# A fused attention, state-space and expert kernel on one core: expert selection moved into the first stage

## What is computed

```
x = x + xattn(layernorm(x), ctx)      # q, k from ctx; softmax(q k^T); x_m = logits attention^T
x = x + ffn16(layernorm(x))           # router scores -> top 2 of 16 experts per token, silu(g) * u, down
x = x + mamba(ctx, layernorm(x))      # in_proj, conv of 4 taps, silu, dt = softplus(...), scan over tokens
x = x + ffn8(layernorm(x))            # two experts of 8, chosen for all tokens

scores = x @ router_w                 # [tokens, 16]
routing_weights, routing_idx = top_k(softmax(scores), 2)   # then normalised to sum 1
dt = softplus(dt_low @ dtp_w + dtp_b)
state = state * exp(dt * A) + (dt * u) * B_t ;  y = sum(state * C_t)
```

## Time and profile before

| | |
|---|---|
| median of 3 runs | 1596.34 us (1596.19, 1596.34, 1598.69) |
| the profiled execution | span 1594.7 us; what lies around a span is not shown by the profile, the median is 1.6 us above it |
| busy share of the span | PE 87%, weight loads 65%, DVE 59%, ACT 45%, POOL 49% |
| chain that ended last, by engine | PE 58%, DVE 22%, issue 10%, ACT 4%, POOL 3%, DMA 3% |
| 0 to 250 us, first stage | 58 us for a batch |
| 250 to 294.5 us, sort | PE idle but for 2 us, DVE busy |
| from 294.5 us | scans and experts, then the third and fourth layer |

### The profile page before, as it was taken

One profiled execution on the slowest core, in us unless ns is written; L12 is line 12 of the kernel. 1 busy time (PEld: TensorE's weight loads), 2 busy tenths in 40 slices (PEclk: granted clock), 3 DMA queues, 4 the chain that ended last, 5 costly groups with the idle time before them and its releaser, 6 DMA issues.

```text
span 1594.7 us, 18873 instructions
## 1 busy us (share of the span) xinstructions
PE 1391.5 (87%) x6080; PEld 1030.4 (65%) x6080; DVE 936.9 (59%) x1186; ACT 709.8 (45%) x1303; POOL 784.0 (49%) x607
## 2 busy tenths in 40 slices
PE   6988983588899989897166999999999999999998
PEld 3535532566666656664166787878787887878786
DVE  2677767999999999998683224241414224241413
ACT  4445433266766776665143333333333333333332
POOL 0000000788888988885631445444544545444442
PEclk9898895699999999999555999999999999999999
DMA  3202214477977987863655900010000100010000
GB/s 105 108 26 81 107 53 165 158 240 257 315 257 234 319 269 264 281 198 125 218 198 203 364 14 0 0 66 1 14 0 13 52 13 0 0 53 0 0 0 26
DMA packets 78202, 191.29 MB, mean 120 GB/s; under 512 B 10856, under 2 KB 15752, under 8 KB 77120
## 3 DMA queue, kind: packets, MB, share of 16 engines
q1 hardware_dynamic: 64832, 157.03, 29.3%
q0 software_dynamic: 6400, 20.98, 4.1%
q10 hardware_dynamic: 6912, 12.59, 2.2%
HBM read 152.55 MB, written 38.01 MB: 119 GB/s over the span
## 4 chain that ended last, share of the span: by engine, by line
PE 58%; DVE 22%; issue 10%; ACT 4%; POOL 3%; DMA 3%; ACTq 0%; SPq 0%; DVEq 0%; POOLq 0%
PE decay L1675 22%; PE bank L1664 21%; DVE decay L1247 11%; DVE S L1256 4%; PE bank L1474 2%; PE decay L1430 2%; PE bank L1437 1%; DVE XH L1114 1%; PE bank L1494 1%; PE bank L1534 1%; PE decay L1484 1%; PE bank L1619 1%; POOL Y L767 1%; PE bank L1561 1%; PE decay L1480 1%
## 5 line engine op out<-in xcount | busy, mean ns | idle before, releaser
L1387 DVE CAST HFH<-HF 128x512 fp32r<-128x512 f32 x128 | 59.0, 461 | 496.7 <-ACT HF L1045 496.7
L815 POOL TENSOR_TENSOR W2L<-W2R,W2H 128x512 fp32r<-128x512 f32 x128 | 172.5, 1347 | 348.2 <-ACT W2H L1040 348.2
L728 POOL TENSOR_TENSOR S<-DTU,Bb 128x1024 f32<-128x1024 f32 x128 | 304.7, 2401 | 25.1 <-DVE row_hot L1229 21.7
L1247 DVE TENSOR_TENSOR_SCAN decay<-decay,S 128x1024 f32<-128x1024 f32 x128 | 292.9, 2288 | 0.5 <-ACT decay L892 0.5
L1664 PE MATMUL bank<-XSH,W1H 128*128 128x512 f32 x512 | 202.9, 396 | 4.2 <-POOL W1L L811 4.2
L1675 PE MATMUL decay<-W2H,HFH 128*128 128x512 f32 x512 | 200.4, 391 | 5.3 <-DVE HFL L1389 5.3
L1664 PE MATMUL bank<-XSH,W1L 128*128 128x512 f32 x512 | 203.0, 396 | 0.0
L1664 PE MATMUL bank<-XSL,W1H 128*128 128x512 f32 x512 | 202.3, 395 | 0.0
L1675 PE MATMUL decay<-W2L,HFH 128*128 128x512 f32 x512 | 199.9, 390 | 0.0
L1675 PE MATMUL decay<-W2H,HFL 128*128 128x512 f32 x512 | 199.7, 390 | 0.0
L811 POOL TENSOR_TENSOR W1L<-W1R,W1H 128x512 fp32r<-128x512 f32 x128 | 171.1, 1337 | 49.6 <-ACT W1H L1031 49.6
(11 more groups left out here) (212 smaller groups left out, 2102.3 us busy)
## 6 DMA issues: line engine op xcount, KB each, us to landing
WGU<-in_L_ffn_gate_w SPq DMA_DIRECT2D x48, 384.0 KB, 3.8
WGU<-in_L_ffn_up_w SPq DMA_DIRECT2D x48, 384.0 KB, 5.1
WD<-in_L_ffn_down_w SPq DMA_DIRECT2D x48, 384.0 KB, 4.9
Bb<-bc_rows SPq DMA_DIRECT2D x32, 512.0 KB, 7.9
Cb<-bc_rows SPq DMA_DIRECT2D x32, 512.0 KB, 9.7
expert_rows<-YT ACTq DMA_DIRECT2D x48, 256.0 KB, 4.2
W1R<-in_L_ffn_w SPq DMA_DIRECT2D x6, 1024.0 KB, 13.9
W2R<-in_L_ffn_w SPq DMA_DIRECT2D x6, 1024.0 KB, 14.1
```

What stands on the lines that cost most here:

```text
L728: pool.tensor_tensor(S[u % NP][:], DTU[:, ds(b, 1), c, :].to_broadcast([P, PAIR, L]), Bb[j][:], ALU.mult).then_inc(dbu_ready, 1)
L815: pool.tensor_tensor(W2L[f % 2][:], W2R[:, ds(e, 1), f, :].rearrange("p e d -> p (e d)"), W2H[f % 2][:].bitcast(F32), ALU.subtract).then_i ...
L1247: dve.tensor_tensor_scan(flat, flat, S[u % NP][:].rearrange("p i l -> p (i l)"), 0.0, ALU.mult, ALU.add).then_inc(scan_done, 1)
```

## The change

- Selection of experts for a batch (top 2, OH, MM, diff) is a function `select(b)`. It is run for batches 0, 1 and 2 in the following batch, between `softmax` and `convolve`, and for batch 3 behind the stage.
- DVE's hardware loop over batches is written out.
- bn_stats of a tile is taken between the additions of x, not behind all four.
- In batch 3 ACT takes the scores ahead of Exp; DVE runs select(3), then softplus(3) without DT and DTU, which come as `step_sizes(3)` behind rf and ahead of row_hot.
- The 16 additions of totals become one `tensor_tensor_scan` with a mask `reset` that is zero at each expert's first tile; PE writes the totals in the order expert, tile.
- SP loads the row pairs 0 to 3 of batch 0 (B and C, eight transfers) in batch 3, two pairs behind `qk_ready`, two behind the turning of the probabilities; U and the pairs 4 to 7 follow where the loads were.
- POOL makes its constants ahead of its waits, and starts the units at `hot_ready` 2, the first product for tile_hot.
- Buffers are allocated in another order, so that the early rows land on the memory of ctxT and XN.

```
@@ transfers (SP)
             def sequence_transfers(b, last):
+                if last:
+                    sp.wait_ge(qk_ready, B)
+                    sp.wait_ge(bc_stored, DMA + DMA)
+                    first_rows(0)
+                    first_rows(1)
+                    sp.wait_ge(t_ready, (B - 1) * 12 + 2 * T)
+                    first_rows(2)
+                    first_rows(3)
                 sp.wait_ge(u_ready, b + 1)
...
-            for j in range(NP):
-                load_b(0, j)
-                load_c(0, j)
-                if j < DC:
-                    load_u(0, j)
+            for j in range(DC):
+                load_u(0, j)
+            for j in range(HP, NP):
+                first_rows(j)
@@ POOL
-            pool.wait_ge(score_copied, B)
-            pool.wait_ge(x1_stored, B * DMA + DMA)
-            pool.wait_ge(xn1_stored, B * DMA + DMA)
-            pool.wait_ge(bc_stored, B * DMA + DMA)
-            pool.wait_ge(dt_ready, B)
...
+            pool.memset(reset[:, :, 0:1], 0.0).then_inc(const_ready, 1)
...
-            pool.wait_ge(hot_ready, 1)
+            pool.wait_ge(x1_stored, B * DMA + DMA)
+            pool.wait_ge(xn1_stored, B * DMA + DMA)
+            pool.wait_ge(bc_stored, B * DMA + DMA)
+            pool.wait_ge(dt_ready, B)
+            pool.wait_ge(hot_ready, 2)
             for u in range(AHEAD):
                 dbu(0, u)
@@ ACT
+            def take_scores(b):
+                wait_apart(act, score_ready, b + 1)
+                act.copy(SC[:, ds(b * T, T), :], PS[6][:, 0:T * E].rearrange("p (t e) -> p t e", t=T)
+                         ).then_inc(score_copied, 1)
...
+                if last:
+                    take_scores(b)
                 act.wait_ge(abs_ready, b * DC + DC)
                 act.activation(ZZ[:], ZZ[:], ACT.Exp, scale=-1.0).then_inc(z_ready, 1)
...
+                if not last:
+                    take_scores(b)
...
-            act.wait_ge(diff_ready, 1)
+            act.wait_ge(diff_ready, B)
@@ DVE
+            def step_sizes(b):
...
+                step.mark(dve.tensor_tensor(DT[:, b], RL[:], ZZ[:], ALU.add))
                 step.wait()
+                dve.tensor_tensor(DTU[:, b], DT[:, b], U[:], ALU.mult).then_inc(dt_ready, 1)
...
+            def select(b):
+
+                ts = slice(b * T, (b + 1) * T)
+                dve.wait_ge(score_copied, b + 1)
+                for t in range(T):
+                    ins = dve.max(M8[:, t, :], SC[:, b * T + t, :])
+                do(ins)
+                for t in range(T):
+                    ins = dve.max_index(I8[:, t, :], M8[:, t, :], SC[:, b * T + t, :])
+                dve.tensor_tensor(diff[:, ts].rearrange("p (t o) -> p t o", o=1), M8[:, :, 1:2], M8[:, :, 0:1],
+                                  ALU.subtract).then_inc(diff_ready, 1)
+                do(ins)
+                for k in range(TOP):
+                    ins = dve.tensor_copy(IF[:, k, :].rearrange("p (t o) -> p t o", o=1), I8[:, :, k:k + 1])
+                do(ins)
+                dve.wait_ge(const_ready, 4)
+                for k in range(TOP):
+                    ins = dve.tensor_tensor(OH[:, k, ts], iota_e[:]..., IF[:, k, :]..., ALU.is_equal)
+                do(ins)
+                dve.tensor_tensor(MM[:, ts], OH[:, 0, ts], OH[:, 1, ts], ALU.add).then_inc(mask_ready, 1)

             def sequence_dve(b, last):
                 softmax(b)
+                if b:
+                    select(b - 1)
                 convolve(b)
...
+                add_x(0)
+                add_x(1)
+                measure(0)
+                measure(1)
+                add_x(2)
+                measure(2)
+                add_x(3)
+                step.mark(measure(3))
                 dve.wait_ge(xn1_stored, b * DMA + DMA)
+                layernorm(X1A, XN1, b * 2 + 2, var_ready, rstd_ready, xn1_ready, measured=True)
                 positive_part(b)
                 if not last:
                     layernorm_x(b + 1)
-                softplus(b)
+                    softplus(b)
+                    step_sizes(b)

             layernorm_x(0)
-            with step.loop(B - 1, 3 * DC + 2 + 4 + 2 * T) as b:
-                sequence_dve(b, False)
-            sequence_dve(B - 1, True)
+            for b in range(B):
+                sequence_dve(b, b == B - 1)
+
+            select(B - 1)
+            softplus(B - 1)
...
-            do(dve.memset(PX[:, 0, :], 0.0))
-            totals = DOWN[:, 0:NT * E].rearrange("p (t e) -> p t e", t=NT)
-            for t in range(NT):
-                do(dve.tensor_tensor(PX[:, t + 1, :], PX[:, t, :], totals[:, t, :], ALU.add))
+            do(dve.tensor_tensor_scan(PX[:].rearrange("p e t -> p (e t)"), reset[:].rearrange("p e t -> p (e t)"),
+                                      DOWN[:, 0:NT * E], 0.0, ALU.mult, ALU.add))
...
             do(dve.scalar_tensor_tensor(rf[:], jf[:], -float(P), posf[:], ALU.mult, ALU.add))
+            step_sizes(B - 1)
             dve.tensor_tensor(row_hot[:], iota_r[:]..., rf[:]..., ALU.is_equal).then_inc(hot_ready, 1)
@@ PE
-            pe.matmul(DOWN[:, 0:NT * E], ones[:], MM[:].rearrange("p t e -> p (t e)"), start=True,
-                      stop=True).then_inc(rank_ready, 1)
+            pe.matmul(DOWN[:, 0:NT * E].rearrange("p (e t) -> p e t", e=E), ones[:], MM[:].rearrange("p t e -> p e t"),
+                      start=True, stop=True).then_inc(rank_ready, 1)
```

More of the change, by code:

```diff
@@ L183, in build_program @@
-        q.close()
+        PR = sb(s, "PR", [P, T, L])
+        QKT = sb(s, "QKT", [P, 2, L])
+        X1A = sb(s, "X1A", [P, T, DM])
+        XN1 = sb(s, "XN1", [P, T, DM])
+        XP = sb(s, "XP", [P, DC, L + TAPS - 1])
+        RL = sb(s, "RL", [P, DC, L])
+        ND = sb(s, "ND", [P, DC, L])
+        ZZ = sb(s, "ZZ", [P, DC, L])
+        XH = sb(s, "XH", [P, DC, L])
+        xdb = sb(s, "xdb", [XD, L])
+        XB = sb(s, "XB", [P, T, DM])
+        XNT = sb(s, "XNT", [P, K, L])
+        ATT = sb(s, "ATT", [P, K, L])
@@ L184, in build_program @@
+        MM = sb(s, "MM", [P, NT, E])
         s.close()
         m = ExitStack()
+        BC = [[sb(m, f"Bb{j}", [P, PAIR, L]), sb(m, f"Cb{j}", [P, PAIR, L])] for j in range(HP)]
         S = [sb(m, f"S{j}", [P, PAIR, L]) for j in range(NP)]
[L188 to L189 removed]
+        BC += [[sb(m, f"Bb{j}", [P, PAIR, L]), sb(m, f"Cb{j}", [P, PAIR, L])] for j in range(HP, NP)]
+        Bb, Cb = [bc[0] for bc in BC], [bc[1] for bc in BC]
@@ L702, in _ @@
             rstd_of(2 * B, var_ready, rstd_ready)
-            pool.wait_ge(score_copied, B)
-            pool.wait_ge(x1_stored, B * DMA + DMA)
-            pool.wait_ge(xn1_stored, B * DMA + DMA)
-            pool.wait_ge(bc_stored, B * DMA + DMA)
-            pool.wait_ge(dt_ready, B)
-            pool.affine_select(out=tri[:], in_=ones[:], compare_op=ALU.is_gt, fill=0.0, base=0,
+            step.mark(pool.memset(tri[:], 0.0))
+            step.mark(pool.memset(reset[:], 1.0))
+            step.wait()
+            pool.affine_select(out=tri[:], in_=tri[:], compare_op=ALU.is_gt, fill=-1.0, base=0,
                                pattern=[[1, P]], channel_multiplier=-1).then_inc(const_ready, 1)
+            pool.memset(reset[:, :, 0:1], 0.0).then_inc(const_ready, 1)
             pool.iota(iota_j[:], pattern=[[1, SLOT_TILES]], base=0, channel_multiplier=0,
@@ L1061, in _, with layernorm @@
             dve.wait_ge(small_loaded, SMALL_LOADS * DMA)
[L1062 to L1067, removed]
+            def layernorm(src, dst, count, ready, got, done, measured=False):
+                if not measured:
+                    for t in range(T):
+                        ins = dve.bn_stats(stats[:, t, :], src[:, t, :])
+                    step.mark(ins)
+                step.wait()
                 for t in range(T):
@@ L1126, in softplus @@
             def softplus(b):
-                dt, dtu = (a_[:, ds(b, 1)].rearrange("p b c l -> p (b c) l") for a_ in (DT, DTU))
                 dve.wait_ge(z_ready, b + 1)
@@ new lines, in do @@
+            def do(ins):
+                step.mark(ins)
+                step.wait()
+            def select(b):
[4 more added lines that the diff above has]
+                do(ins)
+                for t in range(T):
+                    ins = dve.max_index(I8[:, t, :], M8[:, t, :], SC[:, b * T + t, :])
[7 more added lines that the diff above has]
+                for k in range(TOP):
+                    ins = dve.tensor_tensor(OH[:, k, ts], iota_e[:].rearrange("p (o e) -> p o e", o=1).to_broadcast([P, T, E]),
+                                            IF[:, k, :].rearrange("p (t o) -> p t o", o=1).to_broadcast([P, T, E]),
+                                            ALU.is_equal)
+                do(ins)
+                dve.tensor_tensor(MM[:, ts], OH[:, 0, ts], OH[:, 1, ts], ALU.add).then_inc(mask_ready, 1)
```

127 lines of the change are left out of this document (45 added, 82 removed).

## The result

The changed kernel takes 1598.58 us (median of 17 runs, 1595.94 to 1600.95). The kernel before, timed beside it on the same chip, takes 1594.20 us (17 runs, 1588.29 to 1598.69). The ratio is 1.0025, with a 95% interval of 1.0015 to 1.0035: slower by 2.4 to 5.6 us, the middle just above the 0.2% that I had called the least that can be told. The forecast was 1596.1 us and "within 0.2%". The time lies in the range, the sign does not agree.

What follows compares the result with a forecast made beforehand. No engine is busy throughout; the first stage's and sort's chain of waits decides. Tail -10.7, selection +5.7, clock +3.4, router +1.4 give -0.2: 1594.7 - 0.2 + 1.6 = 1596.1 us, own range 1593 to 1599, wider range 1591 to 1600.

Steps and rivals of the forecast that it cites:

- Selection, 1.9 us a batch: First stage: selection between softmax and convolution delays PE by 1.9 us in batches 1 to 3, +5.7 us in all.
- New wait of 2.6 us, falls of 1.7 us, two of three: Attention: PE idles 2.6 us before its second half; the clock falls, 1.7 us each, in two of three batches, +3.4.
- 5.7 + 3.4 = 9.1: First stage: 5.7 us for three selections on PE's path and 3.4 us for two falls of the clock.
- Router, +1.4: Last batch's router: its products take 4.09 us or 7.01 at half clock, now on the path; the middle, +1.4 us.
- Tail, -10.7: Sort, from the last router's end to the first scan: R + 33.6 in place of R + 44.3, -10.7 us.
- R: The end of the router's products in the last batch, 250.21 us before, from which the tail is counted.
- the bound that I did not take: tile_hot to first scan: upper bound of 3.7 us, if the second product goes before POOL's first S; 2.7 was taken.
- Statistics, order on ACT: First stage: bn_stats between the additions gain nothing; last batch: scores before Exp put softplus at R + 3.6, selection hidden.
- First rows, "nothing": SP's loads in batch 3: eight transfers moved ahead of u_spill, none on the path, so worth nothing.
- rival 3: Second stage's start: the gather behind eight S becomes the bound, up to 4.2 us later against the scans; 1598.2, chance 0.10.
- my half of 4.2 us, +2.1: Second stage's start: half of the gather's largest delay against the scans, 1596.1 + 2.1 = 1598.2 us.
- Rival 4: Sort: tile_hot takes 9.95 us even without POOL beside it, for its own cause; +7.0 us, 1603, chance 0.02.

Runs made afterwards that it cites:

- e3: The changed kernel with five dummy products on PE ahead of the second half of attention, in all batches; 1603.57 us, 1.0043 of the kernel before.
- e7: The changed kernel with two dummy products on PE ahead of the second half of attention, in all batches; 1603.96 us, 1.0047 of the kernel before.
- e1: The changed kernel with the selection of the batch before moved ahead of softmax; 1588.94 us, 0.9952 of the kernel before.
- e2: The changed kernel with the selections of batches 0 to 2 put behind the last batch's normalisation; 1588.31 us, 0.9951 of the kernel before.
- e11: The changed kernel with POOL's first S started behind row_hot again, not behind tile_hot's first product; 1598.95 us, 1.0021 of the kernel before.
- e10: The changed kernel with the bn_stats behind all additions of x again; 1599.44 us, 1.0019 of the kernel before.
- e8: The changed kernel with Exp ahead of the scores on ACT in the last batch again; 1597.98 us, 1.0011 of the kernel before.
- e9: The changed kernel with the first rows of B and C loaded behind the last batch again; 1600.64 us, 1.0025 of the kernel before.
- e5: The changed kernel run again without an edit; 1599.81 us, 1.0019 of the kernel before.
- e4: The changed kernel with POOL gathering the first two expert tiles behind six units, not eight; 1596.22 us, 1.0001 of the kernel before.

## Why the prediction was wrong, point by point

- *Selection, 1.9 us a batch:* 1.95 (MAX8 at 158.00, convolution at 159.95). Right.
- *New wait of 2.6 us, falls of 1.7 us, two of three:* 2.67 and 2.55 us, +1.70 and +1.65 us, two of three. Right in size; over the seven executions with this first stage it is 15 falls behind 16 such waits. That they could be had back by filling the wait was not in the prediction, and e3 and e7 did not win it. From the first router to the last it is +8.0 us against before, where 5.7 + 3.4 = 9.1 was forecast; against e1 and e2, which differ by the place of the selection alone, +10.8 and +9.6. Seven executions of the same first stage or nearly the same have their falls in different batches and lines, and sums within 0.6 us. The Trainium skill (TensorE: Matmul & The Clock Gate, The HAM clock gate) has it that the steps aren't tied to the kernel's start and vary between runs; the traces agree as to where the falls sit, while the sums hardly vary.
- *Router, +1.4:* it took 4.27 us, near the full-clock 4.09 of the earlier trace rows. In other executions it took 4.16 to 5.08, or 7.01. A spread, as said.
- *Tail, -10.7:* -10.2. Softplus R + 3.5 (forecast 3.6), ex R + 10.6 (10.6; the terms written down, 7.2 + 3.2, give 10.4, without the 0.2 of ex itself), PO R + 12.0 (12.0), row_hot R + 23.8 (23.5), first scan R + 34.2 (33.6). The 0.6 us between 33.6 and 34.2 are the bound that I did not take: DVE idles 2.35 us ahead of the first scan, a whole S long, so the first S seems to have run only when the second product was done (287.92 + 1.83 = 289.75), though POOL's row begins at 289.14. By the Trainium skill's rule (SBUF — State Buffer, Who interferes with whom), cited for that bound, the two exclude each other; the trace agrees, and so does e11: apart, tile_hot takes 3.65 us and an S 2.41; with the two side by side, tile_hot takes 9.95 and an S 2.65 on the mean of the eight.
- *Statistics, order on ACT:* nothing (e10, e8). Right.
- *First rows, "nothing":* right against the tail before, wrong as a step of this change. The prediction looked at who released POOL's first S and not at the third, and did not carry the loads' new start behind DT into the same line (e9).
- **The step that failed** stands in the first part: "From the first scan on, scan and read-out fill DVE, so an earlier first scan moves all that follows". They did not fill DVE even before: it waited 3.1 and 0.7 us for the first tiles' gating. An earlier first scan moves what follows only if the first expert tile moves as well. What the runs showed in its place is rival 3: eight S ahead of the gather, the slots ready before POOL is, DVE waiting for the first tile, +2.4 us. I gave it 0.10 because of "four more scans to do meanwhile". The scans were done, and the decay behind the expert's work on ACT was then late. That my half of 4.2 us, +2.1, comes near is in part luck. POOL's lead over the first scan went from 9.7 to 2.95 us, of which its wait of 2.69 us for the slots took up a part, but its eight S took 19.3 us in place of 21.45, so against the scans the gather came 1.9 us later (16.29 behind the first scan, 14.40 before) and not 4.2. On top came the fall of the clock in the first tile's up-projection, +2.2, which the prediction did not have.
- *Rival 4:* its +7.0 is too much. By its own rows (9.95 behind R + 27.9) the first scan would have come at R + 37.9, 4.3 later than forecast; e11, where tile_hot does take 9.95, has R + 38.05.
- *The sum.* In the profiled execution the errors cancel: at the first scan the forecast was -0.2 and it was -2.45 (R +7.7 in place of +10.5, the tail -10.2 in place of -10.7); then +2.4 came back. The medians are 3.4 to 4.4 us apart (e5 and the first comparison). The two profiled executions hide this: the changed one, 1596.39 us, lies 2.2 below its own median, and the one before, 1596.34, lies 2.1 above that of its 17 runs. The rest beyond the gather, 1 to 2 us, I can't give to a step: e4 gives back all of the difference, and e5's span is 2.2 us longer than the changed kernel's first trace, though its last scan starts only 0.3 later (749.1 against 748.8), so most of that arises behind the scans, where nothing was edited. The forecast was also anchored on three runs of the kernel before; its medians here went from 1594.2 to 1596.9.

## What to carry to other kernels

Before counting a shorter prologue as gained, follow every engine's lead over the one that it feeds: the time by which POOL is ahead is a resource, and a start that comes earlier for the consumer alone uses it up. Work put on an engine that idles elsewhere belongs into that idle time, not just into the same stage: three selections of 1.95 us cost 9.6 to 10.8 us of the first stage ahead of the convolution, the clock's falls included, and nothing to be seen ahead of softmax (170.2 us between the routers, 173.1 in the kernel before). Where two states of a clock mix, compare the stretch between two milestones over several executions, not one product's time.

## What the runs showed of the hardware

- In the changed kernel, e4, e5 and e8 to e11, an idle stretch of PE of 2.5 to 2.7 us ahead of the second half of attention was followed by a fall of the granted clock to 0.50 for part of the next products, +1.5 to +1.7 us on 7.13, 15 times of 16 (the exception is e5, batch 3: 2.54 us, none at once). After the five stretches of 1.5 to 1.8 us there was none directly.
- With that stretch filled by products (e3, e7) no second half showed a fall. In e3 the other lines ran as in the changed kernel, and the dummies' excess took what was saved; in e7's one trace L1529 and routers ran at half clock instead.
- Ahead of the first expert tile PE was idle 1.2 us in the kernel before and 0.9 in e11, waiting for ACT's U, and the tile's up-projection took 2.85 and 2.82 us. In the eleven other executions that wait was 2.2 to 3.7 us, and the up-projection took 4.31 to 5.49.
- Two DVE operations with two inputs in SBUF, beside POOL's multiplication: 5.99 us in place of 1.83 for the same pair (e11 against the changed kernel), and POOL's own eight from 19.3 to 21.2 us. DVE's loss is the larger one, and yet the kernel's time did not show it.
